# Third stage of a two-layer decoder kernel: a new order of the two lanes' steps on four engines

## The reference

```python
# x: (32, 128, 128) after L0 attention and L0 cross attention (first stage)
x = _layernorm(x + _L0_ffn_ref(x, ...))        # quantised: relu(w1 x + b1), then w2
# L1 attention, a gated delta rule with 16 heads of 64, chunks of 64 tokens:
for step in chunk:
    S = S * a_t[:, :, None]
    S = S + (b_t * k_t)[:, :, None] * (v_t - kTS)[:, None, :]
x = _layernorm(x + _L1_attn_ref(x, ...))       # short conv, silu, Q, K, V, alpha, solve, output gate
x = _layernorm(x + _L1_xattn_ref(x, ctx, ...)) # 16 heads of 8
x = _layernorm(x + _L1_ffn_ref(x, ...))        # relu squared, projection, five spike thresholds
```

## Time and profile before

| | us |
|---|---|
| median of 3 runs | 2652.53 |
| lowest and highest run | 2648.38 to 2654.99 |
| profiled execution, first to last instruction | 2659.3 |
| third stage in it | 1721.9 |
| one round of it | 103.8 |

### The profile page before, as it was taken

How to read it: one execution, slowest core, us unless ns; L and a number is a source line. 1 busy time by engine, 2 the same in 40 slices (tenths; PEclk the granted TensorE clock), 3 DMA queues, 4 the chain that set the end, 5 groups by cost and what they waited for, 6 DMA issues and landing times.

```text
span 2659.3 us, 93159 instructions
## 1 busy us (share of the span) xinstructions
PE 2338.5 (88%) x41310; PEld 1738.7 (65%) x41314; DVE 1532.4 (58%) x3564; ACT 1679.5 (63%) x4172; POOL 295.0 (11%) x396
## 2 busy tenths in 40 slices
PE   3888889888888479999989999999999999999997
PEld 2666666666666257767767667777676676676775
DVE  3565656656565546555555665556656656655563
ACT  2778778777877245655656656556656566565563
POOL 0101010110100000110011001101110110011010
PEclk8999999999999689999999999999999999999997
DMA  3000000000000100000000000000000000000000
GB/s 111 8 9 9 8 9 9 10 8 9 9 8 7 50 7 9 7 7 7 6 9 7 7 9 7 7 6 6 9 8 6 9 7 7 9 7 7 6 6 4
DMA packets 55339, 29.77 MB, mean 11 GB/s; under 512 B 24224, under 2 KB 53216, under 8 KB 54944
## 3 DMA queue, kind: packets, MB, share of 16 engines
q1 hardware_dynamic: 50624, 21.90, 3.0%
q10 hardware_dynamic: 4320, 1.97, 0.3%
HBM read 18.60 MB, written 5.24 MB: 9 GB/s over the span
## 4 chain that ended last, share of the span: by engine, by line
PE 38%; DVE 13%; ACT 11%; issue 2%; DMA 0%; SPq 0%; DVEq 0%
PE bank L1130 5%; PE bank L1197 2%; PE bank L1327 2%; ACT PT L1382 2%; DVE h L1530 2%; DVE zels L462 2%; PE bank L358 2%; PE bank L1260 2%; ACT zels L1382 2%; DVE m L458 2%; PE bank L1246 1%; DVE h L1643 1%; PE bank L1320 1%; PE bank L1170 1%; PE bank L1229 1%
## 5 line engine op out<-in xcount | busy, mean ns | idle before, releaser
L1040 POOL TENSOR_TENSOR PT<-zels,unit 128x512 f32<-128x512 f32 x160 | 203.7, 1273 | 1472.3 <-ACT zels L1382 1284.1
L358 PE MATMUL bank<-w_gate,ident 128*128 128x256 f32 (+3 forms) x960 | 314.5, 411 | 0.0
L458 DVE TENSOR_REDUCE m<-bank 128x4 f32<-128x512 f32 x384 | 251.6, 683 | 39.7 <-PE bank L383 19.2
L393 PE MATMUL bank<-ident,zels 128*128 128x128 f32 x1536 | 226.3, 282 | 34.3 <-ACT zels L429 26.9
L1382 ACT ACTIVATE zels<-bank 128x512 f32<-128x512 f32 (+1 forms) x256 | 142.6, 573 | 158.8 <-PE bank L1246 82.6
L393 PEld LDWEIGHTS bank<-ident,zels 128*128 128x128 f32 x1536 | 168.3, 142 | 83.4 <-ACT zels L429 38.4
L437 ACT ACTIVATE PT<-bank 128x512 f32<-128x512 f32 x384 | 206.1, 629 | 3.8 <-PE bank L393 2.9
L1382 ACT ACTIVATE PT<-bank 128x512 f32<-128x512 f32 x256 | 147.8, 598 | 89.7 <-PE bank L1303 47.7
L433 ACT ACTIVATE zels<-zels 128x512 f32<-128x512 f32 x256 | 162.7, 646 | 55.5 <-DVE zels L462 55.1
L429 ACT ACTIVATE zels<-bank,m 128x128 f32<-128x128 f32 x512 | 148.0, 389 | 64.7 <-DVE m L458 64.7
L462 DVE TENSOR_TENSOR zels<-bank,m 128x512 f32<-128x512 f32 x256 | 177.0, 692 | 8.9
(11 more groups left out here) (293 smaller groups left out, 5125.7 us busy)
## 6 DMA issues: line engine op xcount, KB each, us to landing
ctxT<-in_ctxT_dram SPq DMA_DIRECT2D x64, 48.0 KB, 1.8
x_after_cross_attention<-x SPq DMA_DIRECT2D x32, 64.0 KB, 1.5
h<-x_after_cross_attention SPq DMA_DIRECT2D x8, 256.0 KB, 2.8
xin<-x_after_cross_attention SPq DMA_DIRECT2D x32, 64.0 KB, 1.8
out_dram<-xn SPq DMA_DIRECT2D x32, 64.0 KB, 1.6
x<-in_xT_dram ACTq DMA_DIRECT2D x30, 64.0 KB, 1.8
input_integers<-xq SPq DMA_DIRECT2D x8, 128.0 KB, 2.0
xq<-input_integers SPq DMA_DIRECT2D x32, 32.0 KB, 1.8
```

What stands on the lines that cost most here:

```text
L358: mm(bank[:, 0:cols], ident[:, :], w_gate[:, :, :].rearrange("p a b -> p (a b)")[:, 0:cols], start=True, stop=True)
L393: last = xp(b[u][:, j * P:(j + 1) * P], n.zels[:, u, j * P:(j + 1) * P], ident[:, :])
L458: dve.tensor_reduce(top, scores, AX_X, ALU.max if t == "y" else ALU.min).then_inc(ph.dve[s], ph.DV.step(s, f"{t}max{u}"))
L1040: pool.tensor_tensor(n.TI[:, k % 2, :, :], (n.PT0, n.PT1)[k % 2][:, :, 1, :], unit[:, :].unsqueeze(1).broadcast_to([P, NP, DK]), ALU.add)\
```

## The change

The four rows of the third stage's table are replaced. No step, instruction, buffer or filler is added or removed. The row of GpSimd gives the same cyclic order of its ten operations as before, only the cut between rounds lies elsewhere; the orders of PE, ACT and DVE differ.

```diff
         CSLOTS = slots_of(CSTAGES, {
-            "pe": (35, "100101001010001101011011010111010101000110010000101101110101110011101010110100110101",
-                   "10101011001100101010010101100100011000"),
...
+            "pe": (35, "100100101010111000110101101000101100101000110100101011110110010101100011101101010110",
+                   "01110111001011001000110111000001010100"),
```

More of the change, by code:

```diff
@@ L1008, in decoder @@
         CSLOTS = slots_of(CSTAGES, {
-            "pe": (35, "100101001010001101011011010111010101000110010000101101110101110011101010110100110101",
-                   "10101011001100101010010101100100011000"),
[L1011 to L1016, removed]
+            "pe": (35, "100100101010111000110101101000101100101000110100101011110110010101100011101101010110",
+                   "01110111001011001000110111000001010100"),
+            "act": (35, "100101001111100010001110100000101100101100100110111001110110010001011111001100110110",
+                   "01110111010010101100110010000010010101"),
+            "dve": (36, "010000110111001011001110000101010010010101101011011001100110110010101101101011010001",
+                   "11101111001100001010100111000100001110"),
+            "pool": (30, "101011100010001110010111111101001011010010001111011000110010001101101000110100100110",
+                   "11111100000010000011010101101011100100"),
         }, TAILS)
```

## The result

The changed kernel takes 2715.15 us (median of 4 runs, 2710.05 to 2720.29) against 2653.76 us before (2648.38 to 2657.95): a ratio of 1.0236, 95% interval 1.0216 to 1.0257. It is slower, as forecast, but by 61 us where 24 were forecast, and 15 us above the range.

The account below looks back on a forecast made before the run. PE was taken as the bound, busy 96.49 of 103.80 us in a third-stage round. The median 2652.5 us plus 0 for the waits and 24 for the clock gave 2676.5 us, range 2640 to 2700.

Parts of the forecast that it names:

- The waits: PE's waits in a third-stage round: 5.1 us go, 5.2 come, so even at 0.1 us, -0.8 to +0.8.
- term (5): New waits at lane b's layer norms between solve steps, both lanes' key norms, lane a's end transpose: 0.3, 0.4, 0.2 us.
- L1158's: New PE idle time between lane a's conv and alpha, waiting for DVE's L1559: 1.6 us in every round.
- The clock: Idle time at lane a's alpha halves the clock in half of the rounds: eight falls, 3.0 us each, 24 us.
- term (4): Lane b's output norm has nothing in front any more: 0.4 us more wait, and 0.2 more at the gate behind.
- What comes: The list of new PE waits, (1) to (5), at alpha, lane b's solve, query and norms: 5.2 us a round.
- the small stalls of PE's instruction supply: In the faster rival: stalls that might fall into remaining waits, helping a round gain 1.1 to 1.5 us.
- The clock holds: Rival: no falls in the third stage, 2640 to 2666 us, likeliest no change; chance of no fall 0.28.
- Falls nearly always: Rival: fourteen falls at 3.4 us in the third stage, 48 us more, 2700 us; chance 0.15.
- Faster: Rival: five waits close better than counted and the clock holds, 2632 us; chance of a faster result 0.15.
- ACT's order: Rival: lane a's quantised activations behind lane b's last solve step on ACT delay fc, 0.5 us a round, 8 us.

Follow-up runs that it names:

- the second profile: The changed kernel run once more, unaltered, for a second profiled execution: 2705.87 us, ratio 1.0198 to the kernel before.
- The two pairs: Changed kernel without and with 8 more fillers before lane a's alpha (2715.15, 2671.89 us); kernel before with alpha place new, without and with (2704.91, 2675.93 us).

## Why the prediction was wrong in size

**The waits: right.** Nearly every wait it named came or went, at its place, most within 0.2 us; of term (5) only the key norms (L1192) have a row. L1158's was 1.9 instead of 1.6: DVE took up L1152's result 0.26 us behind its end (1598.70 - 1598.44) and not 0.05, as it was busy with the first tap (L1528) until then, and the filler ended 0.64 us behind L1152 instead of 0.75. Their sum was forecast at 0.1 us a round, ±0.8. Measured by the two rounds at full clock, less their waits on issue, it is (104.40 - 1.0) - (103.80 - 0.8) = 0.4 us. By the constants of all rounds it is 103.62 - 103.54 = 0.1, and 0.0 in the second profile.

**The clock: right in size.** A fall was priced at 3.4 us for 6.8 at half clock, less 0.4, so 3.0, or 0.44 us for each. The two pairs give 0.46 and 0.50, the rounds 0.39. The Trainium skill, "TensorE: Matmul & The Clock Gate", Terms, puts the penalty of the lower clock at half of its time; the pairs come near that, the rounds stay below it. Forecast were falls in half of the rounds, 8 x 6.8 = 54 us more at half clock, 24 us. Measured are 71.8 us more in the first profile and 60.0 in the second, at 0.39 that is 28 and 23. In part that is luck, as the count was too low and the price too high. Two things were not seen. Falls come in 12 of the 15 rounds behind the first in either profile, though 5 of 16 in the one and 11 of 16 in the other are 3.4 us long and not 6.8. And three or four rounds have two, the first at lane b's norm, whose waits (0.7 and 0.8, term (4)) I had priced as waits only.

**The missing term: waits on issue.** This is the step that failed: a term put at nothing. In "What comes" the bunching of the solve steps was costed by the waits for other engines alone. I read PE's waits from one steady round, and its rows on issue, of 0.3 us each, were below the 0.4 at which the list stopped; the whole stage had 22.6 us of them before. The change adds 21.1 us (first profile) or 13.1 (second), and made alone its solve stretch costs 17 us. The prediction mentions "the small stalls of PE's instruction supply" only as something that could fall into other waits and help. That name, here and in the expectations, is a guess at what these waits on issue are.

The account of the third stage, then, with the prices of the rounds: 28.0 (clock, 71.8 x 0.39) + 21.5 (issue, 21.1 x 1.02) + 1.3 (waits for other engines, 16 x 0.08) = 50.8 us for a measured 51.1. For the second profile it is 23.4 + 13.4 + 0.3 = 37.1 for 1757.80 - 1721.90 = 35.9. The forecast had 24 + 0 + 1.6, the last left out of its sum. By the median the loss was 61 us on the first occasion and 51 on the second. The profiled execution of before was a slow one of its kind and that of the change a fast one: the spans lie 5.5 us above and 4.8 below the medians, which makes 61.4 of the spans' 51.1. The profiles account for the 51.1; for the other 10 us no profile was kept.

**The rivals.** "The clock holds" is true of 3 rounds in 15. Idle times of 1.92 us, with matmuls at either side, had a fall with them in 11 rounds of 15. The Trainium skill, "TensorE: Matmul & The Clock Gate", Part 1, has the clock lowered after an idle window; as the prediction read it, the clock would have held, and the traces disagree with that reading. "Falls nearly always", 48 us, was nearer in the count than the forecast, too dear in the price, as many falls are short, and near the measured total only because it had the issue term's share in the wrong place. "Faster" by closed waits had a right half: a round at full clock is about as good as before. "ACT's order" left no row.

**What stays open.** Why falls ahead of `alpha`, at waits of 0.7 and 0.8 us behind L1303's small matmuls, come in some rounds and not in others: they are 5 and 4 in the two profiles of the change, 3 to 5 where the filler removed the others, 7 where the old place stands in the new order. No run filled that place. The third place shown ahead of the prediction, where lane b's solve begins, was not changed alone either; what it adds is known only as the constants of the whole. And what a wait on issue is was argued from its place only (nearly all of these rows are lines of 64x64 matmuls): the runs show what order brings it, not what PE waits for. The Trainium skill, "Runtime: NRT & Kernel Launch", Instruction fetch mechanics, has instruction fetch hidden behind the issue of instructions; if these waits are that fetch, this stage speaks against it with 15.9 to 43.7 us, but no run shows that they are.

## What to carry to other kernels

Price a new order in three sums, not one: the waits for other engines, the clock that idle stretches cost behind them, and the waits on issue where small matmuls are bunched; read each over the whole stage, since a steady round hides the last two. A filler that only takes the place of waiting delayed nothing here and gave back 29 to 43 us, while one that outlasted its wait cost 4.4; a wait of over a microsecond on the engine that sets the pace should be filled, no longer than it is, before it is judged. And a piece of a good order put into another one brings waits that neither has: two parts of a change, measured apart, cost 54 and 17 us where the whole cost 61 or 51, and half of the 54 was waits that the whole does not have. Where a profile holds many rounds of the same work, a line through them prices each loss without a further run.

## What the runs showed that was not expected

The granted clock depended on the length of idle stretches far below the 6.8 us that a fall lasts: with 1.92, 1.06 and 0.20 us in front of the same matmul, 11, 8 and none of the falls lay there. Falls last 3.4 or 6.8 us here, seldom 10.2, and the same program puts them in other rounds when it runs again (1260.1 and 1273.7 us in one profile of the change, 1161.2 and 1376.2 in the other). And the new interleaving of the solve brings 13 to 20 us more of waits on issue with the same 34,272 matmuls in the stage: their order counts, not their number.
